# One mask product per score unit, written ahead of the score products

## The reference

```
qkv = layernorm(x) @ w_qkv.T + b_qkv                 # q, k rotated (rope)
attn = einsum('bhqd,bhkd->bhqk', q, k) * 16 ** -0.5
attn = where(key > query, -inf, attn); attn = softmax(attn)
x = x + layernorm((attn @ v) @ w_out.T + b_out)
h = silu(n @ W1.T) * (n @ W3.T)                      # n = layernorm(x)
x = x + layernorm(fwht(h) @ W2.T)
```

## Time and profile before

| | |
|---|---|
| median of 3 runs | 547.67 us (546.11, 547.67, 552.81) |
| profiled execution: span | 553.2 us; no time of its own is given apart from it |
| PE busy | 452.1 us (82%), 3136 products |
| DVE, ACT, POOL busy | 283.9, 210.4, 163.2 us |
| L411 score products | 256, 89.1 us |
| L413 mask products | 256, 62.8 us |
| L893 maxima | 176, 108.8 us |

### The profile page before, as it was taken

How to read it: one execution, slowest core, us unless ns; L and a number is a source line. 1 busy time by engine, 2 the same in 40 slices (tenths; PEclk the granted TensorE clock), 3 DMA queues, 4 the chain that set the end, 5 groups by cost and what they waited for, 6 DMA issues and landing times.

```text
span 553.2 us, 8654 instructions
## 1 busy us (share of the span) xinstructions
PE 452.1 (82%) x3136; PEld 370.6 (67%) x3136; DVE 283.9 (51%) x676; ACT 210.4 (38%) x302; POOL 163.2 (29%) x280
## 2 busy tenths in 40 slices
PE   1779798987699995988679994989499998975993
PEld 1679555566599874567579873658389875555993
DVE  6653592268425685247525677136835676155114
ACT  5353306722312334833312223853313228721321
POOL 4243003615212213624211212633402216501332
PEclk9989766999669997999769997799879999996996
DMA  8479500002970002001890001100590001000001
GB/s 234 164 154 182 122 0 2 2 1 76 205 137 1 1 2 79 2 0 38 194 185 3 1 0 46 35 1 1 125 244 12 1 0 60 20 1 0 1 1 38
DMA packets 31751, 32.83 MB, mean 59 GB/s; under 512 B 2400, under 2 KB 30816, under 8 KB 31712
## 3 DMA queue, kind: packets, MB, share of 16 engines
q1 hardware_dynamic: 31712, 32.25, 25.1%
HBM read 21.76 MB, written 10.49 MB: 58 GB/s over the span
## 4 chain that ended last, share of the span: by engine, by line
PE 60%; DVE 13%; DMA 9%; issue 7%; ACT 6%; SPq 3%; POOL 1%; DVEq 0%; POOLq 0%; ACTq 0%
PE ps L250 30%; PE ps L424 8%; PE ps L411 7%; PE ps L438 6%; DMA q_t<-qk_scratch 5%; ACT probs L624 4%; PE ps L413 3%; DVE maxima L893 2%; DMA qk_scratch<-qk_s 2%; SPq L291 2%; DMA raw_bias<-in_b_out 1%; PE ps L466 1%; DVE qk_s L856 1%; DVE xy L953 1%; PE ps L383 1%
## 5 line engine op out<-in xcount | busy, mean ns | idle before, releaser
L893 DVE TENSOR_REDUCE maxima<-ps 128x1 f32<-128x384 f32 (+3 forms) x176 | 108.8, 639 | 85.3 <-PE ps L413 83.8
L250 PE MATMUL ps<-xt,w_s 128*128 128x256 f32 x768 | 119.1, 305 | 0.0
L250 PEld LDWEIGHTS ps<-xt,w_s 128*128 128x128 f32 x768 | 106.4, 208 | 0.0
L411 PE MATMUL ps<-k_t,q_t 96*128 96x128 f32 (+3 forms) x256 | 89.1, 399 | 12.9 <-DMA q_t<-qk_scratch 9.7
L763 POOL TENSOR_TENSOR hid_s<-gate,hid_s 128x512 fp32r<-128x512 f32 x32 | 40.9, 1278 | 161.6 <-ACT hid_s L636 161.6
L624 ACT ACTIVATE probs<-ps 128x1280 f32<-128x1280 f32 x64 | 76.8, 1241 | 26.3 <-PE ps L424 25.1
L424 PEld LDWEIGHTS ps<-q_t,k_t 128*128 128x128 f32 x256 | 49.4, 220 | 44.6 <-issue 24.3
L424 PE MATMUL ps<-q_t,k_t 128*128 128x512 f32 (+3 forms) x256 | 62.1, 376 | 17.1 <-issue 12.5
L411 PEld LDWEIGHTS ps<-k_t,q_t 96*128 96x128 f32 x256 | 56.5, 223 | 17.8 <-DMA q_t<-qk_scratch 10.5
L250 PE MATMUL ps<-w_s,hid_s 128*128 128x256 f32 x384 | 64.0, 306 | 2.5 <-POOL hid_s L763 2.5
L413 PE MATMUL ps<-mask_b,ident_b 128*128 128x128 bf16 x256 | 62.8, 250 | 0.0
(11 more groups left out here) (116 smaller groups left out, 509.0 us busy)
## 6 DMA issues: line engine op xcount, KB each, us to landing
qk_scratch<-qk_s SPq DMA_DIRECT2D x16, 512.0 KB, 4.5
k_t<-qk_scratch SPq DMA_DIRECT2D x48, 128.0 KB, 4.6
q_t<-qk_scratch SPq DMA_DIRECT2D x24, 256.0 KB, 6.8
xa<-in_x SPq DMA_DIRECT2D x4, 512.0 KB, 8.4
xy<-in_x SPq DMA_DIRECT2D x4, 512.0 KB, 3.4
out<-xy SPq DMA_DIRECT2D x8, 256.0 KB, 2.2
o_t<-in_w SPq DMA_DIRECT2D x1, 1024.0 KB, 10.4
raw_w<-in_w SPq DMA_DIRECT2D x1, 1024.0 KB, 8.8
```

What stands on the lines that cost most here:

```text
L250: ins = eng.matmul(o, lhs(i), rhs(j), start=first and n == 0, stop=last and n == 2, skip_group_check=skip)
L411: pe.matmul(o[:, i * keys:(i + 1) * keys], q_t[0:QK_ROWS, h // 2, qt * P:qt * P + P], k_t[0:QK_ROWS, h, 0:keys], start=(i == 0), stop=Fals ...
L893: dve.tensor_reduce(maxima[:, qt % 2, heads[0]:heads[0] + len(heads)], src, AX.X, ALU.max)\
```

## The change

Each score unit begins with one mask product, the identity times the mask repeated for each of its heads, written to the last 128 columns of every head's part of the bank (an output with a step, and a moving operand with a repeated dimension). It carries the start flag. The score products follow, all without the start flag, and the last of them signals `scored`. Of a unit's products of mask one remains: 4 x 128 columns become one of 512, 2 x 128 one of 256, and where a unit has one head it is still one of 128. The score products have the same operands as before, and the turn units are as they were.

```diff
                 keys = (qt + 1) * P
+                last_keys = o[:, 0:keys * len(heads)].rearrange("p (h n) -> p h n", h=len(heads))[:, :, keys - P:keys]
+                pe.matmul(last_keys, ident_b[:, :], mask_b[:, :].unsqueeze(1).broadcast_to([P, len(heads), P]),
+                          start=True, stop=False, skip_group_check=True)
                 for i, h in enumerate(heads):
-                    pe.matmul(o[:, i * keys:(i + 1) * keys], q_t[0:QK_ROWS, h // 2, qt * P:qt * P + P],
-                              k_t[0:QK_ROWS, h, 0:keys], start=(i == 0), stop=False, skip_group_check=True)
-                    ins = pe.matmul(o[:, (i + 1) * keys - P:(i + 1) * keys], ident_b[:, :], mask_b[:, :],
-                                    start=False, stop=(i == len(heads) - 1), skip_group_check=True)
+                    ins = pe.matmul(o[:, i * keys:(i + 1) * keys], q_t[0:QK_ROWS, h // 2, qt * P:qt * P + P],
+                                    k_t[0:QK_ROWS, h, 0:keys], start=False, stop=(i == len(heads) - 1),
+                                    skip_group_check=True)
                 ins.then_inc(S["scored"], 1)
```

## The result

The changed kernel takes 529.13 us (median of 4 runs, 525.91 to 531.43); the kernel before, on the same chip, 546.89 (4 runs, 541.67 to 552.81). The ratio is 0.9694, 95% interval 0.9638 to 0.9749: 3.1% faster, some 17 us. The forecast was 2.9 us less (544.8), its range ended at 541.5, and "faster by over 2%" had a chance of 0.02. The profiled execution has a span of 528.3 us against 553.2, 24.9 less. Executions of one kernel differ by up to 3.3% here, some with a lower granted clock: the medians in this document take in all of them, the ratios only the faster ones of each kernel, and the profiled executions of the kernel before, e1, f64, f192, g0 and g1 are among the slower.

A forecast was written before the change was run, and what follows sets the result against it. PE was taken to bound the kernel where it has no gaps, chiefly beside three feed-forwards. Savings of 3.47 us less 0.5 for later ends and 0.1 in the first batch gave 2.9: 544.8 us, range 541.5 to 549.7.

The forecast's parts named there:

- faster by over 2%: Whole kernel: over 11 us less, said to need three times the largest effect named; chance 0.02.
- The mechanism of the products: Units beside feed-forwards: merging saves 0.04 us per 4-head unit, 0.12 per 2-head unit, 1.12 per feed-forward.
- The later end of one-head units: One-head units: last product ends 0.054 us later; three of five waits pass it on, 0.16 us per feed-forward.
- the rival that came out slower: All 96 one-head units beside the feed-forwards hand on their later end: 1.8 us slower, 549.5 us; chance 0.06.
- more than five waits: Sign that the prediction is wrong: PE waits for a DVE maximum more than five times per feed-forward.
- The first batch: First batch's units: savings ahead of the 3.03 us DMA wait only lengthen it; a later DVE run costs 0.1 us.
- The short score products: Rival, 4-head units: score products don't wait for their neighbour's load, 2.6 us more saved, 542.2 us; chance 0.12.
- the half-rate mask product: Rival, merged mask products: stepped output runs at half rate, 5.1 us more, 549.9 us; chance 0.07.
- Nothing moves on SP, ACT or POOL but with PE: Whole kernel: no term of their own for these engines in the sum of 2.9 us less.
- The clock beside the feed-forwards: Rival: earlier starts shift PE out of or into a half-clock stretch, 4.5 us, 540.3 or 549.3 us; chance 0.15.

The follow-up runs named there:

- e1: Changed kernel with 40 already satisfied waits on PE ahead of the loop and 40 inside it: 536.5 us, ratio 0.974 to the kernel before.
- f64: Kernel before, products untouched, with 64 already satisfied waits (32 instructions) on PE ahead of the loop: 531.09 us, ratio 0.973.
- f192: Kernel before, products untouched, with 192 already satisfied waits (96 instructions) on PE ahead of the loop: 541.79 us, spread too wide for a ratio.
- g0: Kernel before with 64 already satisfied waits on PE ahead of the loop, run again as a base: 536.38 us, ratio 0.983.
- g1: Changed kernel with 104 already satisfied waits on PE ahead of the loop and 40 inside it: 531.59 us, ratio 0.976 to the kernel before.
- e3: Kernel before with the merged mask product ahead of the score products in the loop's units only, not the first batch's: 534.51 us, ratio 0.983.
- e2: Kernel before with the merged mask product ahead of the score products in the first batch's units only: 537.39 us, ratio 0.981.
- e5: Against the kernel before: one merged mask product per unit, placed behind the score products: 527.42 us, ratio 0.969.

## Why the prediction was wrong

**The mechanism of the products: right, a little small.** Mask product of 512 columns, four score products each waiting for its own load, 2-head units with every load covered: 1.39 and 1.09 us against 1.41 and 1.09. The gain in a feed-forward at full clock was foretold as 1.12 before the later ends; the stage measured 1.5 with them. The first unit behind the DMA wait gave 0.16 and not 0.04 (1.55 to 1.39), the other 4-head ones 0.06 to 0.09.

**The later end of one-head units: cost nothing, 0.16 us per feed-forward was taken.** PE does wait for maxima more often in the changed kernel, 6 + 1 times in the third feed-forward:

```profile
PEld ps L411 <- DVE maxima L895: 2.2, 6, 0.7
PEld ps L406 <- DVE maxima L895: 0.9, 1, 0.9
```

against 1.1 us in four and 0.6 in one. But from the first 384-key unit to `attend` that feed-forward takes 435.99 - 403.43 = 32.6 us, before it was 460.87 - 428.15 = 32.7. So the rival that came out slower had its sign, more than five waits, without its price.

**The first batch: right.** Its gain went into the DMA wait, 4.53 us where it was 3.03:

```profile
59.76 0.29 PE L411 MATMUL ps<-mask_b,ident_b 128*128 128x128 bf16 x1 [4.53 <-DMA q_t<-qk_scratch]
```

**The short score products and the half-rate mask product: both fell.** A 4-head unit with six feed-forward products between would take 1.41 - 0.22 = 1.2 us by the one and 1.41 + 0.21 = 1.62 by the other; it takes 1.39. A stepped output and a repeated input cost nothing that shows.

**The step that failed** is "Nothing moves on SP, ACT or POOL but with PE": the sum had engines and DMA queues and no term for PE's own instruction stream. The change removes 40 instructions from the loop and 40 ahead of it, and with them went 12.5 us of idle time at two jumps, more than four times the 2.9 us of the forecast. The products gave 4.5 us, later ends included, where the sum had 2.9: by them alone the time would have stayed inside the range. Its rows were to be had. The view of waits of the kernel before has it as PE's second longest wait:

```profile
PE ps L383 <- DVE rot L882: 24.2, 12, 2.6
PE ps L424 <- issue: 12.5, 4, 5.0
```

and the 7% "issue" stood in the earlier trace rows. I looked for what each removed product occupied of PE, and took a wait that the profile puts down to nothing as fixed. I saw no way to tell from the trace of before which way 80 instructions fewer would turn it; but it gave the price, 10 to 12.5 us, and a rival "the jump's fetch goes" would have put the range's end at 532 and given "faster by over 2%" a real chance. The 0.02 for that rested on "three times the largest effect that I can name", which was too high as well: 11 us is little more than twice the 5.1 us of the half-rate rival.

The Trainium skill ("Runtime: NRT & Kernel Launch", "Instruction fetch mechanics") says that a taken branch forces a fetch before execution goes on if its target isn't in the current window of two pages, and gives PE's instruction memory as 2048 instructions, refilled in blocks of 256. The trace agrees with the stall (3.91 and 5.00 us idle, 0.47 and 0.43 without it) and with 16 KB packets (0.51 MB in 31). In the window of two the runs differ: a loop of 1,560 instructions, more than six blocks, ran its second and third pass without a packet, and f64 did so with one of 1,600. Nor did a loop that touches eight blocks, which is 2048 instructions, stay: all of these were fetched again, e3's at the first jump only.

**The clock beside the feed-forwards: no sign that the change sets it.** PE stood at half clock beside the first feed-forward for a shorter time in the changed kernel, the 3 us left above. Mean granted clock from 150 to 210 us, third number from the end: first the kernel before, then e2, with the same products in its loop:

```profile
150.00:210.00 60.00, 54.96 (x387) 0.91 0.22 41
```

```profile
150.00:210.00 60.00, 54.13 (x403) 0.98 0.23 46
```

f64 and g0, again with these products, have 0.89 and 0.91. With merged products the changed kernel has 0.97, g1 0.94, e3 0.93 and e5 1.00. So it differs from execution to execution, and the two sets overlap. This is most of what separates the 24.9 us between the two profiles from the 17 between the medians. The clock behind the jumps is another matter: where PE doesn't stand still there, it was at 1.00 in all 19 cases.

## What to carry to other kernels

A wait "issue" at the start of a loop is a price like any other: look for it at each jump back, and look whether the instruction queue brings packets in later passes. Where an edit changes the number of an engine's instructions in a loop or ahead of it, the loop can slip into or out of what the engine keeps, and the time of the edit is then that of the slip; comparing it with the old kernel moved by some idle waits tells the two apart, and here 64 waits alone were worth 13 us. Count in the trace how many instructions such waits make: here it was half as many. Price products by the distance between starts, and read small gains in a stage at full clock: the whole kernel's time doesn't resolve them.

## What was unexpected of the hardware

PE's loop of 1,560 to 1,600 instructions is either kept for all passes (13 packets), fetched again at each jump (31), or at the first jump only (22, e3). By the count above, every loop that touches seven blocks of 256 was kept and every one that touches eight was fetched again, so that 32 instructions of shift, or 40 fewer of length and 40 fewer ahead, decide it. A missed jump cost PE 3.5 to 7 us of idle time: one wait of 3.5 to 5.2 us, and one of 1.7 to 2.6 more where the loop begins five instructions ahead of the border of a block. Why the first varies by as much stays open. The mean granted clock in the 14 us behind it was 0.59 to 0.88. A product with an output in four runs and a repeated input ran as the columns say (1.39 us for the unit, 1.41 by the rule). Whether the merged product behind the score products (527.4 us) is better than ahead of them (529.1 to 529.8) stays open too, within what the runs can tell.
